# New instruction order on all five queues of a fused attention and RWKV kernel, with a 96-column transpose

## What is computed

```python
# layer 0: attention between x_c and x_s
Mn = conv1x1(Wn, bn, inorm(x_c)); Mm = conv1x1(Wm, bm, inorm(x_s))
A = softmax(einsum('bct,bcs->bts', Mn, Mm))
x = conv1x1(Wo, bo, einsum('bcs,bts->bct', conv1x1(Wl, bl, x_s), A)) + x_c
# layer 1: RWKV-6 block, 32 heads of 16, state from the context
xa = ln(x); sx = shifted(xa) - xa
xxx = low_rank(tanh((xa + sx * maa_x) @ maa_w1)) ; xk, xw, xv, xr, xg = xa + sx * (maa_stack + xxx)
w = exp(-exp(time_decay + tanh(xw @ td_w1) @ td_w2)); r, k, v = xr @ Wr.T, xk @ Wk.T, xv @ Wv.T
g = silu(xg @ Wg.T)
# s = k v + w s over time, out = r (u k v + s)
x1 = x + groupnorm(out) * g @ Wo.T
xc = ln(x1); rr = sigmoid(xr2 @ Wfr.T); kk = square(relu(xk2 @ Wfk.T))
return x1 + rr * (kk @ Wfv.T)
```

## Time and profile before

| what | value |
|---|---|
| median of 3 runs | 1889.99 us |
| profiled execution | 1890.35 us |
| its span, first to last instruction | 1888.5 us |
| mean granted TensorE clock | 0.977 of full speed |
| PE, DVE busy | 1785.4, 1743.5 us |
| ACT, POOL busy | 1174.2, 1048.8 us |
| read and written in HBM | 161.91 and 16.78 MB |

### The profile page before, as it was taken

How to read it: one execution, slowest core, us unless ns; L and a number is a source line. 1 busy time by engine, 2 the same in 40 slices (tenths; PEclk the granted TensorE clock), 3 DMA queues, 4 the chain that set the end, 5 groups by cost and what they waited for, 6 DMA issues and landing times.

```text
span 1888.5 us, 35795 instructions
## 1 busy us (share of the span) xinstructions
PE 1785.4 (95%) x12420; PEld 1235.2 (65%) x12420; DVE 1743.5 (92%) x2468; ACT 1174.2 (62%) x2945; POOL 1048.8 (56%) x886
## 2 busy tenths in 40 slices
PE   4788999999999999999999999999999999999855
PEld 2656667676666667666676776666677676667623
DVE  3499999999999999999999999999999999999871
ACT  3545666666666666666666666667666666766422
POOL 1235666556666655666665566665556665664531
PEclk8899999999999999999999999999999999999878
DMA  5233333333333343333333433333344333333310
GB/s 229 63 96 79 96 102 86 104 105 99 90 95 102 85 106 104 103 88 92 102 88 105 102 107 87 90 102 94 99 102 110 88 88 99 102 91 91 101 51 11
DMA packets 81601, 180.99 MB, mean 96 GB/s; under 512 B 18288, under 2 KB 34800, under 8 KB 80400
## 3 DMA queue, kind: packets, MB, share of 16 engines
q1 hardware_dynamic: 59920, 161.93, 32.2%
q10 hardware_dynamic: 21504, 16.78, 2.8%
HBM read 161.91 MB, written 16.78 MB: 95 GB/s over the span
## 4 chain that ended last, share of the span: by engine, by line
PE 49%; DVE 27%; issue 17%; DMA 3%; POOL 2%; ACT 1%; ACTq 0%; DVEq 0%; POOLq 0%; SPq 0%
PE bank L1088 17%; PE bank L1095 6%; DVE A L642 5%; PE bank L1133 5%; DVE S L657 5%; PE bank L1100 4%; DVE A L669 4%; PE bank L1213 3%; PE bank L1107 3%; DVE nmax L543 3%; DVE xf L600 3%; DMA vrep<-v_dram 3%; PE bank L1120 2%; DVE S L648 2%; PE bank L1169 2%
## 5 line engine op out<-in xcount | busy, mean ns | idle before, releaser
L466 POOL COPY S<-s 128x8 f32<-128x8 f32 x256 | 197.6, 773 | 321.9 <-DVE A L669 212.2
L657 DVE TENSOR_TENSOR_SCAN S<-wrep,S 128x512 f32<-128x512 f32 x256 | 354.5, 1385 | 0.7 <-ACT wrep L941 0.6
L669 DVE TENSOR_TENSOR A<-S,rt 128x1024 f32<-128x1024 f32 x256 | 330.9, 1293 | 0.1
L438 POOL TENSOR_TENSOR xf<-xf,xa 128x512 f32<-128x512 f32 x160 | 218.6, 1367 | 188.3 <-DVE xf L600 185.9
L642 DVE TENSOR_TENSOR A<-vrep,kt 128x1008 f32<-128x1008 f32 x256 | 309.6, 1210 | 10.2 <-DMA vrep<-v_dram 4.8
L857 ACT ACTIVATE prob<-bank,nmax 128x512 f32<-128x512 f32 x128 | 87.3, 685 | 249.0 <-DVE nmax L543 249.0
L648 DVE TENSOR_TENSOR S<-A 128x504 f32<-128x504 f32 x256 | 230.4, 910 | 1.2
L408 POOL TENSOR_SCALAR rstd<-mv 128x1 f32<-128x1 f32 (+1 forms) x96 | 71.7, 747 | 243.9 <-DVE mv L564 143.5
L410 POOL TENSOR_TENSOR hrs<-hrs,mhalf 128x32 f32<-128x32 f32 x32 | 200.5, 6266 | 2.7
L894 ACT ACTIVATE bank<-bank,par 128x128 f32<-128x128 f32 x640 | 174.9, 349 | 29.1 <-PE bank L1169 29.1
L1213 PE MATMUL bank<-A,slide 128*32 128x256 f32 x2048 | 166.2, 397 | 14.4 <-DVE A L669 14.4
(11 more groups left out here) (143 smaller groups left out, 3973.8 us busy)
## 6 DMA issues: line engine op xcount, KB each, us to landing
vrep<-v_dram SPq DMA_DIRECT2D x256, 512.0 KB
xc<-x_c SPq DMA_DIRECT2D x32, 256.0 KB, 6.3
xs<-x_s SPq DMA_DIRECT2D x32, 256.0 KB, 9.5
v_dram<-vT ACTq DMA_DIRECT2D x32, 256.0 KB, 7.3
out<-rr ACTq DMA_DIRECT2D x32, 256.0 KB, 6.2
Wv<-big_w SPq DMA_DIRECT2D x1, 1024.0 KB, 6.2
Wk<-big_w SPq DMA_DIRECT2D x1, 1024.0 KB, 8.2
Wr<-big_w SPq DMA_DIRECT2D x1, 1024.0 KB, 10.2
```

The costliest lines, as they stand in the source:

```text
L438: po.tensor_tensor(xf[:, b, :, :], xf[:, b, :, :], xa[:, :, 1:P + 1], ALU.add).then_inc(pool_mid.sem, 1)
L466: po.tensor_copy(S[:, u % 2, :, 0], s0[:, p, k:k + UJ]).then_inc(pool_wkv.sem, 1)
L657: ve_.tensor_tensor_scan(s, wrep[:, u % C, :, :].rearrange("p j t -> p (j t)"), s, 0.0, ALU.mult, ALU.add).then_inc(dve_scan.sem, 1)
L669: ve_.tensor_tensor(out4, s, r, ALU.mult).then_inc(dve_read.sem, 1)
```

## The change

All five `step` lists are ordered anew. Lists of labels, the two bank rings and the SP list follow. On PE, the new order is:

```diff
 FRONT_JOBS
-    "O:1 V:0 Tx:1 W1:1 Mn:0 Wt:1 Mm:0 Mv:1 Mw:1 S0:0 S1:0 S2:0 Vp:1 Mk:1 Mr:1 Mg:1 D1:1 S3:0 Kp:1 "
-    "D2:1 E2:1 Rp:1 T0:0 T1:0 T2:0 G:1 T3:0").split())]
+    "T3:1 O:1 V:0 G:2 Tx:1 Mn:0 Mm:0 W1:1 Wt:1 S0:0 S1:0 Mv:1 Mw:1 Mk:1 Mr:1 Mg:1 Vp:1 S2:0 D1:1 "
+    "D2:1 E2:1 S3:0 Kp:1 Rp:1 T0:0 T1:0 T2:0").split())]
 BACK_JOBS
-    "FK:4 C:3 C2:3 FR:4 FV:4 Tg:3 Wo:3 Tx2:3").split())]
+    "Tx2:4 FK:4 C:3 C2:3 FR:4 FV:4 Tg:3 Wo:3").split())]
```

POOL's list:

```diff
             def step(s, on):
                 b0, b1, b2, b3, b4 = on
+                if b2: mid_add(*b2, 4)
+                if b4: tail_xc20(*b4)
+                if b1: mid_xa0(*b1)
+                if b1: att_rstd1(*b1)
+                if b2: wkv_s0(*b2, 0)
+                if b2: wkv_s0(*b2, 1)
                 if b0: att_rstd(*b0)
                 if b2: wkv_s0(*b2, 2)
-                if b2: wkv_rk2(*b2)
                 if b3: tail_hrs(*b3)
+                if b1: mid_add(*b1, 0)
+                if b2: wkv_rk(*b2)
                 if b2: wkv_s0(*b2, 3)
-                if b1: mid_add(*b1, 0)
                 if b1: mid_add(*b1, 1)
+                if b4: fin_out(*b4)
                 if b2: wkv_s0(*b2, 4)
-                if b4: fin_out(*b4)
                 if b1: mid_add(*b1, 2)
                 if b2: wkv_s0(*b2, 5)
                 if b1: mid_add(*b1, 3)
+                if b2: wkv_rk2(*b2)
+                if b3: tail_rstd(*b3)
                 if b2: wkv_s0(*b2, 6)
-                if b1: mid_add(*b1, 4)
-                if b3: tail_rstd(*b3)
+                if b1: mid_ez2(*b1)
                 if b2: wkv_s0(*b2, 7)
...
```

The second low-rank transpose takes columns 64 to 160 instead of 96 to 160, so that its tile is the full one, and the mix of g moves from partitions 32 to 64 of `txg` and `w2g` to partitions 64 to 96:

```diff
-                pe.transpose(bank_of("Wt")[0:2 * DM, P:2 * P], txn[:, P - DM:P + DM], ident[:, :]).then_inc(pe_mid.sem, 1)
+                pe.transpose(bank_of("Wt")[0:3 * DM, P:2 * P], txn[:, 2 * DM:5 * DM], ident[:, :]).then_inc(pe_mid.sem, 1)
```

In the start, SP loads the first x and context ahead of the constants, Wv has a semaphore of its own, ACT instead of POOL forms head_u (four instructions), and waits on constants that had long been met are taken out of the loops:

```diff
+            sp.dma_start(xc[:, 0, :], x_c[0]).then_inc(x_loaded[0], 16)
+            sp.dma_start(xs[:, 0, :], x_s[0]).then_inc(x_loaded[0], 16)
             sp.dma_start(attw[:, :, :], att_w).then_inc(setup_loaded[0], 16)
             sp.dma_start(par[:, :], params).then_inc(setup_loaded[0], 16)
...
-            for c in range(C):
-                po.tensor_scalar(head_u[:, c, :], head_rep[:, :], col("u", c), None, ALU.mult).then_inc(pool_const, 1)
...
+            eng.wait_ge(pool_const, CONSTS)
+            for c in range(C):
+                sc.activation(head_u[:, c, :], head_rep[:, :], ACT.Copy, scale=col("u", c)).then_inc(act_setup, 1)
```

More of the change, by code:

```diff
@@ L32 @@
 T2 = P // 2
-CONSTS = 14 + C
+CONSTS = 14
 LAGS = 5
@@ L202, in col @@
             return par[:, k:k + 1]
-        setup_loaded = [sem(f"setup_loaded{i}") for i in range(3)]
+        setup_loaded = [sem(f"setup_loaded{i}") for i in range(4)]
         x_loaded = [sem(f"x_loaded{i}") for i in range(2)]
@@ L221, in units @@
             return " ".join(f"{x}{u}" for u in range(U) for x in text.split())
[L223 to L224 removed]
+        dve_att = Steps(sem("dve_att"), "stats aggr nm mx0 mx1 ri0 mx2 mx3 ri1 ri2 ri3 xin xst xag nm1")
+        dve_mid = Steps(sem("dve_mid"), "sx xx mv mw mk mr mg s0m s0c g")
         dve_pre = Steps(sem("dve_pre"), "kw rw")
@@ L360, in step @@
                 if b2: load_vrep(b2[0], b2[2], 1)
-                if b1 and b1[0] + 1 < NB: load_x(b1[0] + 1, 1 - b1[2])
-                if b1: load_s0(b1[0], b1[2])
                 if b2: load_vrep(b2[0], b2[2], 2)
+                if b2: load_vrep(b2[0], b2[2], 3)
+                if b2: load_vrep(b2[0], b2[2], 4)
+                if b0: load_st1(b0[0], b0[2])
+                if b3: load_st0(b3[0], b3[2])
+                if b2: load_vrep(b2[0], b2[2], 5)
             run(step)
@@ L706, in tail_gate @@
             def tail_gate(n, m, p):
+                if n == NB - 1:
+                    eng.wait_ge(dve_mid.sem, dve_mid.count("g", n))
                 eng.wait_ge(act_tail.sem, act_tail.count("oT", n))
@@ L764, in step @@
-                if b1: mid_s0(*b1)
-                if b2: wkv_read(*b2, 1)
[L766 to L771, removed]
+                if b2: wkv_pair(*b2, 2)
+                if b0: att_max(*b0, 1)
+                if b1: mid_mix(*b1, 0)
+                if b0: att_rinv(*b0, 0)
+                if b2: wkv_scan(*b2, 2)
@@ L780, in step @@
[L780 to L787, removed]
+                if b2: wkv_scan(*b2, 3)
+                if b2: wkv_read(*b2, 3)
+                if b1: mid_mix(*b1, 4)
+                if b3: tail_x1(*b3)
+                if b2: wkv_outer(*b2, 4)
@@ L808, in step @@
+                if b2: wkv_scan(*b2, 6)
+                if b2: wkv_read(*b2, 5)
+                if b1: mid_kw(*b1)
+                if b1: mid_s0c(*b1)
+                if b2: wkv_read(*b2, 6)
+                if b0: att_xin(*b0)
+                if b0: att_xst(*b0)
+                if b1: mid_rw(*b1)
+                if b3: tail_mix(*b3, 0)
                 if b2: wkv_outer(*b2, 7)
-                if b2: wkv_scan(*b2, 6)
+                if b0: att_xag(*b0)
+                if b1: wkv_outer(*b1, 0)
@@ L886, in mid_txt @@
                 sc.activation(tx[:, :], bank_of("Wt")[:, 0:P], ACT.Copy)
-                sc.activation(txg[DM:2 * DM, :], bank_of("Wt")[DM:2 * DM, P:2 * P], ACT.Copy).then_inc(act_mid.sem, 1)
+                sc.activation(txg[2 * DM:3 * DM, :], bank_of("Wt")[2 * DM:3 * DM, P:2 * P], ACT.Copy).then_inc(act_mid.sem, 1)
             def mid_bias(n, m, p, f):
@@ L1028, in step @@
-                if b1: mid_txt(*b1)
-                if b0: att_proj(*b0, 1)
+                if b0: att_proj(*b0, 0)
+                if b3: tail_sq(*b3)
+                if b0: att_proj(*b0, 1)
+                if b1: mid_tx(*b1)
+                if b4: fin_kk(*b4)
+                if b1: mid_txt(*b1)
+                if b4: fin_rr(*b4)
+                if b2: decay(*b2, 2)
+                if b0: att_exp(*b0, 0)
                 if b1: mid_bias(*b1, "v")
+                if b0: att_exp(*b0, 1)
@@ L1041, in step @@
+                if b1: mid_bias(*b1, "r")
+                if b1: mid_bias(*b1, "g")
+                if b2: decay(*b2, 3)
+                if b1: mid_v(*b1)
+                if b0: att_exp(*b0, 2)
+                if b1: mid_dt(*b1)
+                if b0: att_exp(*b0, 3)
                 if b4: fin_store(*b4)
-                if b1: mid_dt(*b1)
-                if b1: mid_bias(*b1, "g")
+                if b1: mid_ez(*b1)
                 if b0: att_scale(*b0, 1)
-                if b0: att_exp(*b0, 3)
@@ L1166, in mid_M @@
                         i = MIX.index(f)
-                        w, x_ = (w2g[DM:2 * DM, :], txg[DM:2 * DM, :]) if f == "g" else \
+                        w, x_ = (w2g[2 * DM:3 * DM, :], txg[2 * DM:3 * DM, :]) if f == "g" else \
                             (w2[DM * i:DM * i + DM, :], tx[DM * i:DM * i + DM, :])
```

193 lines of the change are left out of this document (79 added, 114 removed).

## The result

The changed kernel takes 1908.83 us (median of 4 runs, 1907.03 to 1909.55) against 1890.28 us (1888.52 to 1893.34) before: a ratio of 1.0095, 95% interval 1.0077 to 1.0112. It is slower by 1%, outside the range of 1862 to 1904. The profiled execution took 1909.55 us, its span is 1907.8 us.

The account below looks back on a forecast made before the run. PE (54.5 us a step) and DVE (54.2) were both taken as full in a 54.83 us step; -0.08 x 31 steps and -1.7 at the start gave -4 us, so 1886 us, range 1862 to 1904.

Parts of the forecast that it names:

- The path from Wo to the next sum 6: PE's list from Wo through projections, sum 4, O and sum 5 to the next sum 6: 21.1 us.
- add g, pushed into the next step: beside xin: 0: POOL's add of xa to g's mix would run beside DVE's xin and delay DVE by 0 us.
- Beside mix and x1: 0: POOL's add k would run beside DVE's mix and x1 and delay DVE by 0 us.
- PE's need: PE's own work per step: three trips out of the full tile fewer save 0.9 us, 54.5 to 53.6.
- The wait at Wo: PE, ready for Wo at 32.5 us after sum 6 starts, waits a microsecond for fin_y to empty its bank.
- POOL's power for hrs: POOL's addition (1.2 us) and power (5.4 us) take 6.6 us, just fitting the 7.0 us before gn; cost 0.
- Rival 3: PE's clock falls to the lower level in the transposes: 2.2 us more a step, 1955 us; chance 0.02.
- All holds together: DVE delays from POOL's two-input instructions in their new places: 3.5 us a step against 4.2, bounds 2.4 and 4.8.
- The start: PE's head_u wait and ACT's table load leave the path, params land a microsecond later: -1.7 us (0 to -4).
- Rival 2: fin_y holds Wo longer, gn waits for hrs and another add meets a scan: 55.3 a step, 1903 us; chance 0.20.
- Rival 1: PE's saving arrives because fin_y is on time: 53.9 us a step, 1860 us; chance 0.24, half the way 0.15.
- Rival 4: Trips out of the full tile cost nothing by themselves, the old loss was waiting: 1888 us; chance 0.39 with the forecast.

Follow-up runs that it names:

- e5: e1's kernel with Wo in the bank of Tg instead of the bank that fin_y empties: 1883.52 us, ratio 0.9963.
- e11: e5's kernel with POOL's add k behind the next initial-state copy, and DVE's kw and s0c behind xin and its statistics: 1859.3 us, ratio 0.9830.
- e10: e1's kernel with V between sums 5 and 6 on PE, one trip out of the full tile more: 1889.37 us, ratio 1.0002.
- e1: The changed kernel with kw and s0c moved behind read 6 in DVE's list: 1881.24 us in one run.
- e7: e1's kernel with D1 between sums 2 and 3 on PE: 1907.43 us, ratio 1.0082.
- e8: e1's kernel unchanged, timed again in more runs: 1883.29 us, ratio 0.9954.
- e6: e5's kernel with S3 on PE moved ahead of sums 2 and 3: 1883.25 us, ratio 0.9953.
- e2: The changed kernel with fin_y moved in DVE's list from behind outer 3 to between the mixes of w and k: 1929.22 us.

## Why the prediction was wrong

**The path from Wo to the next sum 6 failed, in its last term.** The prediction put it at 21.1 us; it is 22.14 (1053.77 to 1075.91). Term by term: Wo 3.51 against 3.44; D1 to S3 3.64 against 3.7; k and r 7.24 against 7.2; sum 4 with the transposes 2.81 against 2.8; O 3.53 against 3.5; and from sum 5 to sum 6 1.41 against 0.5. The last is 0.64 us of sum 5 and 0.77 of waiting.

**The step behind it is one line: "add g, pushed into the next step: beside xin: 0".** It assumed that add g comes free after read 6. The copy queued ahead of it is released by read 5, whose end comes 0.4 us before read 6 starts, so the add arrives 0.04 us ahead of it. The mechanism was the prediction's own (a POOL instruction on two SBUF inputs shuts out the next such one of DVE), and so was its price: 1.2 us predicted, 1.0 measured. (The rows behind it were read loosely: fin_out and the add do not end with the pairs and the scan beside them, but at 1044.42 and 1050.18 us, 1.1 us ahead of them; the held instruction then runs its own length.) The place was wrong, by one instruction, and it was never asked who would wait if it was. The path to ask along is sum 4, outer 6, pair 6, scan 6, read 5, kw, s0c, read 6: from sum 4's start to read 6's end it takes 7.69 us, and PE's own work from sum 4 to sum 6 6.98. Only 0.3 us of a hold had room there. "Beside mix and x1: 0" for add k was wrong in the same way (read 3 takes 2.02 us); it cost nothing in the changed kernel, since Wo's wait covered it, and became the next wait in e5.

The Trainium skill ("SBUF — State Buffer", Terms, shared port pair) says that DVE and GpSimd take a port pair for a full instruction, and that the loser fully blocks. By that rule read 6 should take its own length and the add's; the trace agrees, 2.22 us against 1.20 and 1.18, with the add's 0.04 us start ahead and some overlap at its ends.

**What was right.**
- *PE's need.* Without its two waits the step has 55.57 - 0.86 - 0.77 = 53.9 us of PE's work, predicted 53.6; e11 runs at 53.95 with PE full. Before it was 54.6, or 54.5 with all of PE's idle time taken off. Three trips fewer gave 0.6 to 0.7, predicted 0.9, at 0.33 us for one in e10.
- *The wait at Wo,* predicted as about 1 us: 0.86.
- *From sum 6 to the shift* 11.78 us, predicted 11.8 (1020.34 to 1032.12 in the step before the one shown); from the shift to fin_y 20.83, predicted 21.0. The second is in part luck, since inside it the terms were others: add w held the gate by 1.0 us (1.67 instead of 0.68) and not outer 3 by 1.2, rk held nothing (predicted 0.6), and mix k waited 0.52 us for ACT's bias (predicted 0.2, for mix v).
- *POOL's power for hrs* is done 6.6 us after its addition begins, as predicted, by two errors that cancel: the addition takes 0.31 us and not 1.2, the power 6.20 and not 5.4.
- *The clock* is 1.00 in the middle with twenty transposes together. Rival 3 is out.
- *The last steps* cost 1.7 us, inside the 3 allowed.

**Signs that did not come.** An outer near 2.3 us and pair 4 near 1.5 were expected, and ez2 stretched. In the changed kernel outer 3 takes 1.20 us and pair 4 0.67; rk2 meets outer 4 (1.41); ez2 takes 0.89 us, before 1.52, and holds nothing, as DVE waits for sum 4 beside it. All holds together are 3.0 us a step (gate 1.0, read 3 0.8, outer 4 0.2, read 6 1.0), predicted 3.5: the sum was near, the places were not.

**The start** gave 0 instead of -1.7. PE no longer waits for head_u, but the parameters land 2.8 us later behind x (6.47 us, before 3.67), not one, as PE's timeline of the changed kernel shows; the first product of a normalised input starts at 11.87 us, before at 11.96.

```profile
6.47 0.79 PE L1074 MATMUL bank<-attw 128*128 128x128 f32 x2 [6.47 <-DMA par<-params]
...
11.87 1.22 PE L1103 MATMUL bank<-prob,attw 128*128 128x512 f32 x1 [1.79 <-ACT prob L834]
```

**The rivals.** Rival 2 has the nearest number (1903, 55.3 a step, for 1908.8 and 55.57) but not the cause. It wanted fin_y to end later than 33.7 us behind sum 6; fin_y ends 33.3 behind it, gn does not wait for hrs, and the loss is on the other half of the loop. Rival 1's number, 1860, is what e11 reaches (1859.3): the gain was there as counted, but it takes four edits (add g off read 6, Wo off fin_y's bank, add k off read 3, add g off s0c), not one add that falls luckily. Rival 4 is out by e10.

**In one sum:** the forecast of 54.75 and the unforeseen 0.77 are 55.5 a step; measured 55.57. e1 takes just that back. What stays open is which part each single trip has in the 0.7 us that PE saved, because e7 was disturbed, and why the first two intervals after the ACT line's start differ by up to 2.6 us among kernels that differ in one place (57.9 against 55.3 in e10 and e8).

## What to carry to other kernels

When a queue of one engine is reordered, place each instruction of an engine that it can hold up by the event that releases it and what is queued ahead of it, not by the name of its neighbour in the list; then for each long instruction it may hit, write down how late that one may be. Here 0.04 us decided over 0.77 us a step, and two short instructions moved past a read turned 1% slower into 0.5% faster. POOL's two-input work is best put where DVE has a run of PSUM or single-input work as long as itself. A wait that disappears and brings nothing (e5, e6) points to a second late event of the same engine: work on that engine's holds and order, not on the order of the one that waits.

## What the runs showed that was not expected

- The hold does not scale with its victim. s0c, 64 columns and 0.22 us by itself, takes 1.20 us behind an add: a short instruction in the wrong place costs as much as a read.
- POOL and DVE take turns, and a full POOL queue holds DVE again and again. In e2 fin_out, a copy of 8 columns and an add stand without a gap from 1006.06 to 1010.03. fin_out stretches outer 3 to 2.28 us; the copy, 0.20 us when undisturbed, takes 1.18 and is done only when outer 3 is; the add, 0.02 us ahead of pair 3, stretches it to 1.69.
- Moving a consumer earlier can cost 1.1% (e2 against the changed kernel) through a second reader that it releases on another engine.
